# Experts: second weight's low half copied per row, image part in two column groups

## What is computed

```python
scores = jax.nn.softmax(jnp.mean(x, axis=1) @ Wg.T, axis=-1)
_, idx = jax.lax.top_k(scores, 1)
sel = idx[:, 0]
h = gelu(jnp.einsum('bth,ehf->betf', x, W1) + b1[None, :, None, :])   # exact gelu
y = jnp.einsum('betf,efh->beth', h, W2) + b2[None, :, None, :]
w = scores * jax.nn.one_hot(sel, E, dtype=scores.dtype)
out = jnp.einsum('beth,be->bth', y, w)                                # E = 3, F = 768, H = 192
```

## Time and profile before

| | us |
|---|---|
| median of 3 runs | 1046.6 (1045.37 to 1047.09) |
| the profiled execution's own time | 1041.93 |
| its span, first to last instruction | 1040.1 |
| expert stage in it | about 874 to 1036 |
| busy over the whole span: PE / DVE / ACT | 709.4 / 883.8 / 711.7 |

### The profile page before, as it was taken

The page is one execution under the profiler, slowest core; times in us unless marked ns, Lnnn a source line. Parts: engine busy times, 40 slices in busy tenths (PEclk is TensorE's granted clock), DMA queues, the critical chain, the costliest instruction groups (busy, mean ns, idle before and its releaser), DMA issues. The chain is left out here.

```text
span 1040.1 us, 22682 instructions
## 1 busy us (share of the span) xinstructions
PE 709.4 (68%) x5955; PEld 482.6 (46%) x5956; DVE 883.8 (85%) x2422; ACT 711.7 (68%) x1376; POOL 168.9 (16%) x274
## 2 busy tenths in 40 slices
PE   3872396747888366666776676666645385999997
PEld 3552144424555233433443343343323254989896
DVE  5898986888888889999999999999978864666766
ACT  0254364957888699888888989899955294445453
POOL 5851500006555000000000000000003530000000
PEclk9995598988999687788777778878756597999999
DMA  8000000001111111111111111111012004355452
GB/s 255 3 2 0 0 1 1 0 0 38 37 37 37 33 29 25 24 23 23 23 29 24 24 23 25 24 23 24 13 62 105 18 1 151 126 193 203 154 199 89
DMA packets 84272, 54.71 MB, mean 53 GB/s; under 512 B 53705, under 2 KB 83177, under 8 KB 83977
## 3 DMA queue, kind: packets, MB, share of 16 engines
q1 hardware_dynamic: 83208, 54.11, 17.1%
q0 software_dynamic: 1024, 0.13, 0.2%
HBM read 11.90 MB, written 3.76 MB: 15 GB/s over the span
## 5 line engine op out<-in xcount | busy, mean ns | idle before, releaser
L1358 DVE SCALAR_TENSOR_TENSOR expo<-expo,con,pow 128x153 f32<-128x153 f32 x480 | 146.1, 376 | 0.8 <-ACT expo L1267 0.8
L1141 PE MATMUL at_rem<-word,ident_half 128*128 128x459 f16 x160 | 66.0, 412 | 102.9 <-ACT expo L1267 102.1
L1267 ACT ACTIVATE expo<-at_rem,con 128x459 f32<-128x459 f32 x160 | 95.2, 639 | 14.2 <-PE at_rem L1142 13.5
L953 DVE TENSOR_REDUCE rs_ends<-rs_banks 128x770 f32 (+1 forms) x96 | 91.3, 960 | 14.5 <-PE rs_banks L924 12.8
L873 ACT ACTIVATE rs_banks<-rs_banks 128x770 f32<-128x770 f32 x96 | 76.2, 798 | 25.3 <-PE rs_banks L916 24.0
L1223 ACT ACTIVATE word<-at_banks 128x459 uint8<-128x459 f32 x160 | 80.9, 560 | 10.7 <-PE at_banks L779 10.6
L1401 DVE CUSTOM_DVE_ANT_0 weight_top<-weight_top,line 128x2448 uint16<-128x2448 uint16 x64 | 86.2, 1346 | 2.1 <-ACT line L1259 2.1
L1141 PEld LDWEIGHTS at_rem<-word,ident_half 128*128 128x128 f16 x160 | 15.7, 98 | 152.9 <-ACT expo L1267 148.3
L1259 ACT ACTIVATE line<-weight_top 128x1224 f32<-128x1224 f32 x64 | 74.0, 1158 | 15.2 <-DVE weight_top L1386 15.0
L774 PE MATMUL at_banks<-pick,row_top 128*128 128x459 bf16 x160 | 73.4, 459 | 11.0 <-ACT word L1223 4.0
L1907 ACT ACTIVATE qk<-e_p,b1s 128x153 f32<-128x153 f32 x192 | 58.7, 391 | 29.8 <-PE e_p L1868 28.5
(11 more groups left out here) (390 smaller groups left out, 2089.8 us busy)
## 6 DMA issues: line engine op xcount, KB each, us to landing
qk<-vt SPq DMA_DIRECT2D x64, 384.0 KB, 3.1
rs_kb<-qk SPq DMA_DIRECT2D x128, 28.7 KB, 1.9
kb<-qk SPq DMA_DIRECT2D x128, 28.7 KB, 1.9
patches<-in_patches SPq DMA_DIRECT2D x4, 768.0 KB, 10.0
vi<-vt SPq DMA_DIRECT2D x32, 96.0 KB, 2.0
out<-vi SPq DMA_DIRECT2D x32, 96.0 KB, 1.8
pj_w<-in_w SPq DMA_DIRECT2D x1, 2304.0 KB, 8.4
qb<-qk SPq DMA_DIRECT2D x128, 6.0 KB, 1.8
```

Source lines behind the costliest of these rows:

```text
L953: v.tensor_reduce(ends[:, :, n, 5 * b:5 * b + 5], banks[:, slot(u, b), :, 0:5 * W].rearrange("p i (t n) -> p i t n", n=W), AX, ALU.max).th ...
L1141: pe.matmul(out, identh[:, :], bank(word, b).bitcast(F16), start=True, stop=False)
L1267: act.activation(bank(ex, b), rem[:, (u + b) % 2, 0:3 * N], ACT.Square, scale=2.0 ** 24, bias=c(5)).then_inc(sq_done, 1)
L1358: ins = v.scalar_tensor_tensor(ex[:, t, :], ex[:, t, :], c(7), pw[:, t, :].bitcast(BF16), ALU.add, ALU.mult, accum_out=tot[:, t:t + 1])
```

## The change

- The low half of the second weight, `w2l`, of the chosen expert is copied for each row into one of four slots `wl`: two in a new tile, two in a free part of `line`. It is a third DMA in `weights`, of 6 x 192 bfloat16 (2304 bytes) a partition. From row 4 on it waits for `y_acc` of row n-4. `w_in` now counts three DMAs.
- The image part still has 12 matmuls, but of two kinds in turn. High weight: stationary operand `BOTH` (64 columns), into `p3[0:64]`. Low weight, from `wl[slot]`: stationary operand `TAIL`, the high halves alone (32 columns), into `p3[64:96]`. Each kind accumulates by itself. The product low x low is no longer computed for the image tokens.
- `collect` adds a third slice, `p3[64:96]`, to the image tokens: one more instruction on 32 partitions, with a wait for the one ahead of it. `i_half` now counts two a row.

```diff
-    HI, BOTH, LO = slice(0, NT), slice(IW, IW + 64), slice(N + 32, N + 32 + NT)
+    HI, BOTH, LO, TAIL = slice(0, NT), slice(IW, IW + 64), slice(N + 32, N + 32 + NT), slice(IW, N)
...
+        wl_own = sb("e_w2_low", [P, 2, FT, C], BF16)
+        wl_line = m["line"][:, :, :].rearrange("p a b -> p (a b)")[:, 2 * FT * B:2 * FT * B + FT * C].bitcast(BF16).rearrange("p (u f c) -> p u f c", u=2, f=FT)
+        wl = [wl_own[:, 0, :, :], wl_own[:, 1, :, :], wl_line[:, 0, :, :], wl_line[:, 1, :, :]]
...
                     for i, w in enumerate((w1h, w1l)):
                         sp.dma_start(ws[:, u, i, :, :], w[:, :, e, :]).then_inc(w_in[u], 16)
+                    if not (isinstance(n, int) and n < SLOTS):
+                        wait_apart(sp, y_acc, n - SLOTS + 1, k.passed)
+                    sp.dma_start(wl[u], w2l[:, e, :, :]).then_inc(w_in[u], 16)
...
-                    pe.wait_ge(w_in[kk], (n - kk) * 8 + 32)
+                    pe.wait_ge(w_in[kk], (n - kk) * 12 + 48)
...
-                    parts = [(w, f) for f in range(FT) for w in (w2h, w2l)]
-                    for b, (w, f) in enumerate(parts):
-                        mm = pe.matmul(p3[0:64, u, 0:C], gs[:, u, f, BOTH], w[:, e, f, :], start=(b == 0), stop=(b == 2 * FT - 1))
+                    for f in range(FT):
+                        pe.matmul(p3[0:64, u, 0:C], gs[:, u, f, BOTH], w2h[:, e, f, :], start=(f == 0), stop=(f == FT - 1))
+                        mm = pe.matmul(p3[64:96, u, 0:C], gs[:, u, f, TAIL], wl[slot][:, f, :], start=(f == 0), stop=(f == FT - 1))
                     mm.then_inc(y_acc, 1)
...
-                    v.wait_ge(i_half, n + 1)
-                    v.tensor_tensor(yi[r, :], p3[32:64, u, 0:C], yi[r, :], ALU.add).then_inc(i_bias, 1)
+                    v.wait_ge(i_half, n * 2 + 1)
+                    v.tensor_tensor(yi[r, :], p3[32:64, u, 0:C], yi[r, :], ALU.add).then_inc(i_half, 1)
+                    v.wait_ge(i_half, n * 2 + 2)
+                    v.tensor_tensor(yi[r, :], p3[64:96, u, 0:C], yi[r, :], ALU.add).then_inc(i_bias, 1)
```

## The result

The changed kernel takes 1079.12 us (median of 4 runs, 1078.16 to 1080.22); the kernel before, run beside it, 1045.98 (1044.38 to 1047.09). The ratio is 1.0322, with a 95% interval of 1.0307 to 1.0337: +33.1 us, where +29.1 was predicted. The profiled execution of after has a time of 1080.22 us and a span of 1078.4.

What follows compares the result with a forecast made beforehand. The prediction held TensorE (4.72 us a row) and VectorE (4.76) level as bounds; 33.6 for shape changes, minus 6.1 waits, plus 1.2 first load and 0.4 last collect gave +29.1 on 1046.6: 1075.7 us, range 1053 to 1083.

Steps and rivals of the forecast that it cites:

- TensorE and VectorE level, TensorE takes over: Expert stage: TensorE 4.72 and VectorE 4.76 us a row before; after the edit TensorE's 5.77 exceeds VectorE's 5.14.
- the 6.1 us of waits: TensorE's waits between first and last image matmul before the edit, 6.1 of 151.2 us, said to vanish.
- ScalarE loop: Table reload, split, second and first product over two rows: 9.25 us, 4.62 a row; 5.2 after the edit.
- The price of a change of shape (0.095): Image part on TensorE: each change of matmul shape costs 0.095 us, 11 more a row, 1.05 us a row.
- Run together or drain: Image matmuls of differing shapes: TensorE drains (chance 0.50, 1075.7 us) or column groups overlap (chance 0.33, 1059 us).
- The whole run-out (0.165 a change): Rival: each image matmul runs out its whole 0.25 us, 0.165 a change, +53 us, 1099; chance 0.05.
- The added addition: VectorE's third slice in collect: 0.38 us a row, VectorE's chain from 4.76 to 5.14.
- The first load, +1.2: At the first row nothing covers the third transfer, so the stage starts 1.2 us later (0.7 to 1.9).
- SyncE's queue: SyncE issues for 1.9 of 4.8 us a row; the added transfer costs one more issue, some 0.7 us.
- Late weights in every fourth row: Behind image stores TensorE's start is due up to 1.9 us later every fourth row; slower rows pay it back.
- The last collect, +0.4: The added VectorE addition lengthens the last collect at the end of the stage by 0.4 us.
- The rival at 1059: Column groups run together whatever their shapes; VectorE sets the pace at 5.14 a row, 1054 to 1065; chance 0.33.

Runs made afterwards that it cites:

- hoist_after: Changed kernel with VectorE's load of the expert's number moved from collect to the head of the step: 1080.38 us, ratio 1.0338.
- add_only: Kernel before plus one more 32x192 VectorE addition a row into a spare tile, with the changed kernel's waits: 1059.17 us, ratio 1.0129.
- hoist_before: Kernel before with VectorE's load of the expert's number moved from collect to the head of the step: 1044.46 us, ratio 0.9987.
- pairs: Changed kernel with the image matmuls ordered high, high, low, low, so five changes of size inside the image part: 1059.19 us, ratio 1.0130.
- equal64: Changed kernel with the low weight's matmuls also 64 columns wide, into partitions 64 to 127, so all sizes are equal: 1060.67 us, ratio 1.0144.
- copy_only: Kernel before plus the third transfer a row and its waits, with TensorE still reading the resident weight: 1051.62 us, ratio 1.0049.
- stores_on_act: Changed kernel with equal matmul sizes, second bias on TensorE, TensorE's number load later, output stores on ScalarE in a four-row loop: 1038.58 us, ratio 0.9925.
- hoist_equal64: Changed kernel with equal matmul sizes and VectorE's load of the expert's number moved to the head of the step: 1059.57 us, ratio 1.0137.

## Why the prediction was right, and where its terms were off

- **TensorE and VectorE level, TensorE takes over.** Right. Behind the first row TensorE waits for no other engine, as the vanishing of the 6.1 us of waits requires, and hoist_after shows that VectorE's load is off the path. That the two were level before is borne out by add_only (12 us for one addition) and hoist_before (2.5 us of stage for a load of 1.04 us a row moved out of VectorE's way). The prediction's ScalarE loop adds up to 9.24 and not 9.25 for two rows; nothing hangs on it.
- **The price of a change of shape (0.095).** Right mechanism, too small. It is 0.11 here, by after and pairs alike, so the image part grew by 1.22 and not 1.05 us: 32 x 1.22 = 39.0 instead of 33.6. This is 5.4 us more, the largest error in the sum. The estimate was made from changes to and from 128 columns, which give 0.095; the pair of the edit had only one row, behind a matmul of 25 columns, which gave 0.07 and would have been worse. 39.0 - 6.1 = 32.9, and from the first image matmul to the last the trace has 1072.6 - 888.7 = 183.9 against 151.2: +32.7.
- **Run together or drain: open before, settled by equal64.** The trace of before couldn't part change of size from overlap of columns, and the forecast took one side at a chance of 0.50, so the number also rests on that choice. Now it is parted: equal sizes on other partitions run together, 64 beside 32 columns doesn't in any of these runs. The Trainium skill, TensorEngine Tiling (Array Packing), Key Properties, holds that a change of mode drains TensorE; the trace agrees that a change costs, 0.11 us a time. How far the engine empties isn't seen: the next matmul starts 0.195 us behind the last, inside its recorded 0.26. The Trainium skill, TensorE: Matmul & The Clock Gate, Part 3, describes matmuls on distinct column strips as concurrent with no condition on size; equal64 agrees (0.01 us apart), after and pairs don't, and the measurement decides.
- **The whole run-out (0.165 a change).** Refuted: 0.11.
- **The added addition.** Its own cost (0.38, measured 0.38 to 0.39) was right, and that it hides in the forecast's case too. The rival's use of it, 5.14 a row, was too small: 5.22 in add_only, +12.1 us instead of about +9.
- **The first load, +1.2.** It came to 0.74, the issue alone: the third transfer lands in 3.08 us from its start, as the second did in 3.10. The three overlap, so the landing of the third adds nothing. This step took the bandwidth of the first pair as a limit, which it wasn't. (It also set 295 KB beside 768, which count 1000 and 1024 bytes; in the latter the copy has 288.)
- **SyncE's queue.** This step failed, though it didn't decide here. It counted the issues (1.9 of 4.8 us a row) and left out the load of the number (median 0.56 before, 0.87 in copy_only) and the address work between; SyncE was busy some 3.7 a row before and needs 5.10 with the copy. The added issue was put at 0.7 and costs 0.86. Had the image part become shorter, as in the rivals, this would have been one of two bounds above the old pace. Late weights in every fourth row, expected as a loss that slower rows pay back, never show in the chain of after between 885 and 1030.
- **The last collect, +0.4.** Right: from the last image matmul's start to the end of the stage 2.8 us, before 2.4.
- **The rival at 1059.** Its time was good for the three kernels with a short image part (1060.67, 1060.20, 1059.19), of which only equal64 runs its groups together, for a partly wrong reason: it put VectorE's addition at +8.5 and late transfers at +3; the addition alone gives the 12. How addition and copy combine in equal64 (12.1 and 4.6 alone, 13.6 together) wasn't parted.

The signed sum: 29.1 + 5.4 (change of shape) - 0.5 (first load) = 34.0, beside 33.7 in the profiles and 33.1 in the medians.

## What to carry to other kernels

In these runs matmuls on disjoint output partitions overlapped where their sizes were the same and not where they differed: pad the smaller one up to the larger, or sort them so that the size changes once, before counting on column groups. Before adding an issue or an instruction to a tuned loop, add up each sequencer's whole row, register loads and address work included; an engine with no busy time on the page was 0.6 to 1.2 us a row from being the bound here. And where three engines lie within half a microsecond, one edit pays only when the others are relieved with it: here column groups of equal size lost 1.4%, still lost 0.25 to 0.5% with VectorE relieved, and gained 0.75% once SyncE (and with it ScalarE's table) was relieved too.

## What the runs showed of the hardware

- A change between 128*64 and 128*32 costs 0.11 us beside the stream, about the same both ways (989.67 - 989.47 and 989.86 - 989.67, less 0.085) and whether the matmuls alternate (after) or go in pairs. The loads of the stationary operand point to why: inside a stream of one size a load starts some 0.07 us ahead of its own matmul, and after a change it starts with it. TensorE's weight loads in before, inside the image part, and in after, at the same place:
```profile
986.34 0.11 PEld L1884 LDWEIGHTS e_p<-vbd,e_gs 128*64 128x64 bf16 x1
```
```profile
989.67 0.09 PEld L1890 LDWEIGHTS e_p<-e_w_low,e_gs 128*32 128x32 bf16 x1
```
  The first belongs to the matmul at 986.41, the second to the one at 989.67. That this is the cause is read from these rows, not tried by itself.
- Loading one register from SBUF takes a sequencer 0.27 us (SyncE, stores_on_act) to 1.17 us (VectorE, hoist_equal64): in SyncE's rows above the median is 0.56 before and 0.87 in copy_only. On VectorE it starts behind the start of the instruction ahead of it, by 0.1 us at the least in the 28 loads of hoist_equal64's chain, so its place in the program hides little of it.
- SyncE's sequencer can bound a loop, through the landings that it brings late: three copies with an address from a register (0.69, 0.64, 0.52), 0.36 to 0.50 for a store, 1.8 for four, and the number's load came, with the address work between them, to 5.10 us a row (copy_only).
